# Main neighbour table written in 24-slot pieces in place of eight-slot pieces, in a four-layer GNN and expert kernel

## What is computed

```
x = x + gat2(layernorm(x), src, dst)            # two attention layers over the 100,000 edges, dense by counts
x = x + experts8(layernorm(x))
x = x + layernorm(x) @ W(edge_weight, src, dst) # a 256 x 256 matrix scattered from weights
x = x + experts4(layernorm(x), edge_index)      # gate: 4-head attention over 65,536 other edges
x = x + feature_attention(layernorm(x), src, dst)
x = x + experts6(layernorm(x))
x = x + gat8heads(layernorm(x), src, dst)       # 8-head attention over the 100,000 edges
x = x + experts8b(layernorm(x))
```

## Time and profile before

| | us |
|---|---|
| three timed runs | 5290.30, 5306.82, 5312.11 |
| median | 5306.82 |
| the profiled execution, its own time | 5308.64 |
| span of the profiled execution | 5307.1 |
| mean granted clock of PE in it | 0.876 of full |

### The profile page before, as it was taken

The page is one execution under the profiler, slowest core; times in us unless marked ns, Lnnn a source line. Parts: engine busy times, 40 slices in busy tenths (PEclk is TensorE's granted clock), DMA queues, the critical chain, the costliest instruction groups (busy, mean ns, idle before and its releaser), DMA issues. The chain is left out here.

```text
span 5307.1 us, 71457 instructions
## 1 busy us (share of the span) xinstructions
PE 3317.8 (63%) x17311; PEld 2482.2 (47%) x17312; DVE 3019.0 (57%) x7503; ACT 1600.5 (30%) x2745; POOL 2063.6 (39%) x1895
## 2 busy tenths in 40 slices
PE   0440036499698695277771699868345567777677
PEld 0430036487586584255550244356234445555455
DVE  8886648588588556133335754442444555565563
ACT  0232024376475121133330454322101222222221
POOL 1136300200200252656551200026377877777662
PEclk9999999899898796588885899979677788898899
DMA  0311125443452322211123554422443333333241
GB/s 31 74 19 44 13 82 232 169 153 104 170 159 85 111 67 91 88 27 33 33 38 108 200 170 158 165 91 67 129 91 86 88 86 83 82 84 84 78 76 28
DMA packets 326382, 501.17 MB, mean 94 GB/s; under 512 B 152614, under 2 KB 241005, under 8 KB 324168
## 3 DMA queue, kind: packets, MB, share of 16 engines
q1 hardware_dynamic: 193750, 259.75, 15.6%
q0 software_dynamic: 83888, 189.73, 13.7%
q10 hardware_dynamic: 48578, 49.98, 2.8%
HBM read 367.16 MB, written 137.35 MB: 95 GB/s over the span
## 5 line engine op out<-in xcount | busy, mean ns | idle before, releaser
L2393 POOL DMA_INDIRECT l3a_got<-rows,l3a_idx x832 | 1003.3, 1206 | 356.1 <-issue 257.5
L2469 PE MATMUL ps<-l3a_v,ident 128*128 x2032 | 592.9, 455 | 476.8 <-DVEq L2596 395.3
L2469 PEld LDWEIGHTS ps<-l3a_v,ident 128*128 128x128 f32 x2032 | 452.5, 228 | 614.5 <-issue 522.0
L1659 PE MATMUL ps<-l0a_all_rows,l0a_w 128*128 128x257 f32 x2500 | 559.5, 384 | 38.1 <-DVE l0a_w L1768 37.8
L1659 PEld LDWEIGHTS ps<-l0a_all_rows,l0a_w 128*128 128x128 f32 x2500 | 473.9, 191 | 124.3 <-issue 54.3
L2831 POOL DMA_INDIRECT l1a_got<-rows,l1a_idx x352 | 351.2, 998 | 248.8 <-DVEq L3033 130.0
L2069 PE MATMUL ps<-l2a_table,l2a_count 128*128 128x512 bf16 x1875 | 409.7, 382 | 38.1 <-ACT l2a_count L1994 38.1
L2419 ACT ACT_TABLE_LOAD x90 | 115.5, 1283 | 750.7 <-issue 459.4
L2854 PE MATMUL ps<-xt,l1w_w 128*128 x640 | 225.8, 506 | 169.3 <-ACT l1a_h L2909 74.2
L2069 PEld LDWEIGHTS ps<-l2a_table,l2a_count 128*128 128x128 bf16 x1875 | 183.9, 98 | 264.0 <-issue 46.6
L2590 DVE TENSOR_TENSOR l3a_v<-l3a_got,l3a_p_kept x127 | 291.6, 2296 | 0.0
(11 more groups left out here) (1019 smaller groups left out, 6446.8 us busy)
## 6 DMA issues: line engine op xcount, KB each, us to landing
l0a_held<-counts SPq DMA_DIRECT2D x130, 640.0 KB
counts<-count_held SPq DMA_DIRECT2D x13, 3200.0 KB
l2a_held<-counts SPq DMA_DIRECT2D x65, 640.0 KB
l3a_got<-rows,l3a_idx POOLq DMA_INDIRECT x832
l_y<-l1a_y_sb ACTq DMA_DIRECT2D x20, 640.0 KB
l2a_table<-rows SPq DMA_DIRECT2D x16, 640.0 KB, 5.1
l2a_state<-l1a_fresh ACTq DMA_DIRECT2D x1, 9984.0 KB
l2a_seen<-l2a_state POOLq DMA_DIRECT2D x12, 768.0 KB, 6.0
```

The costliest lines, as they stand in the source:

```text
L1659: ins = pe.matmul(sums_of(n, k, D + 1), w[:, at, k * P:(k + 1) * P], all_rows[:, at, 1:RW], start=(at == 0), stop=(at == HI - 1))
L2393: pool.indirect_dma_start(out=got[:, at:at + RW], out_offset=None, in_=rows[:, :], in_offset=bass.IndirectOffsetOnAxis(ap=idx[:, a, k:k + ...
L2469: ins = pe.matmul(totals, c.ident[:, :], rows_now[:, k, :, :].rearrange("p h d -> p (h d)"), start=(k == 0), stop=(k == ADDED - 1))
```

## The change

`write_table` takes the graph's `fewest` as its piece width. For gate that is 8, as before; for main it is 24. The closing piece has the same width. `whole_row`, the most pieces in a chunk, becomes 64 // 24 = 2 for main. `ell` keeps 24 slots ahead of the 64, in place of 8, and the spare area and the table have room for wider pieces. As 24 is no power of two, `fill` no longer shifts to get the number of pieces: it adds up comparisons (size >= 24, size >= 48), which makes two for main and eight for gate.

```diff
-        self.whole_row = WIDE // SLOTS
+        self.whole_row = WIDE // fewest
...
-        m.ell, m.past = sb("main_ell", [P, NT, SLOTS + WIDE], I32), sb("main_past", [P, NT, WIDE])
+        m.ell, m.past = sb("main_ell", [P, NT, m.fewest + WIDE], I32), sb("main_past", [P, NT, WIDE])
...
         def write_table(eng, s, odd, emptied=None):
+            width = s.fewest
...
                         with eng.Fori(0, n_units) as u:
-                            eng.dma_start(s.table[:, bass.ds(to + u * SLOTS, SLOTS)],
-                                          s.ell[:, bass.ds(t, 1), bass.ds(SLOTS + u * SLOTS, SLOTS)].rearrange("p o s -> p (o s)")).then_inc(s.stored[odd], 16)
+                            eng.dma_start(s.table[:, bass.ds(to + u * width, width)],
+                                          s.ell[:, bass.ds(t, 1), bass.ds(width + u * width, width)].rearrange("p o s -> p (o s)")).then_inc(s.stored[odd], 16)
...
-                    eng.dma_start(s.table[:, bass.ds(to, SLOTS)],
-                                  s.ell[:, bass.ds(t, 1), bass.ds(at, SLOTS)].rearrange("p o s -> p (o s)")).then_inc(s.closed, 16)
+                    eng.dma_start(s.table[:, bass.ds(to, width)],
+                                  s.ell[:, bass.ds(t, 1), bass.ds(at, width)].rearrange("p o s -> p (o s)")).then_inc(s.closed, 16)
...
-                        ch.add(dve.tensor_copy(s.full_i[:, :], last[:, 0, :]))
-                        ch.add(dve.tensor_tensor(s.ends[:, :], last[:, 0, :], left[:, :], ALU.is_equal))
-                        ch.add(dve.tensor_tensor(last[:, 1, :], last[:, 1, :], spare[:, :], ALU.subtract))
+                        ch.add(dve.tensor_tensor(last[:, 1, :], dest[:, :], last[:, 0, :], ALU.add))
+                        ch.add(dve.tensor_scalar(row[:, 0:NT], last[:, 0, :], float(width), None, ALU.is_ge))
                         ch.join()
...
+                        ch.add(dve.scalar_tensor_tensor(last[:, 1, :], last[:, 1, :], -float(width * (c.NT + 1)), s.ends[:, :], ALU.add, ALU.mult))
+                        for u in range(2, s.whole_row + 1):
+                            ch(dve.scalar_tensor_tensor(row[:, 0:NT], last[:, 0, :], float(u * width), row[:, 0:NT], ALU.is_ge, ALU.add))
...
-                        ch.add(dve.tensor_copy(s.ell[:, :, 0:SLOTS], s.ell[:, :, WIDE:SLOTS + WIDE]))
+                        ch.add(dve.tensor_copy(s.ell[:, :, 0:width], s.ell[:, :, WIDE:width + WIDE]))
...
-    columns_of = lambda edges, fewest: edges + (fewest + 2 * SLOTS) * NT + 5 * WIDE
+    columns_of = lambda edges, fewest: edges + 3 * fewest * NT + 5 * WIDE
```

More of the change, by code:

```diff
@@ L134, in __init__ @@
         self.last_entry = entries.shape[0] - 1
-        self.whole_row = WIDE // SLOTS
+        self.whole_row = WIDE // fewest
         self.columns = table.shape[1]
-        self.trash = self.columns - WIDE - 2 * SLOTS * c.NT
+        self.trash = self.columns - WIDE - 2 * fewest * c.NT
         self.chunks = -(-edges // WIDE)
@@ L160, in allot @@
         self.moved = sb("moved", [P, SLOTS, NT])
-        self.full_i, self.last, self.ends = sb("full_i", [1, NT], I32), sb("last", [1, 2, NT]), sb("ends", [1, NT])
+        self.last, self.ends = sb("last", [1, 2, NT]), sb("ends", [1, NT])
         self.last_i = sb("last_i", [1, 2, NT], I32)
@@ L215, in build_graphs @@
         g.raw = part_of(c.xt, NT * P, NT * ENTRY).bitcast(I32).rearrange("p (t e) -> p t e", e=ENTRY)
-        g.ell = part_of(five, 0, NT * (SLOTS + WIDE)).bitcast(I32).rearrange("p (t e) -> p t e", e=SLOTS + WIDE)
-        g.past = part_of(five, NT * (SLOTS + WIDE), NT * WIDE).rearrange("p (t e) -> p t e", e=WIDE)
+        g.ell = part_of(five, 0, NT * (g.fewest + WIDE)).bitcast(I32).rearrange("p (t e) -> p t e", e=g.fewest + WIDE)
+        g.past = part_of(five, NT * (g.fewest + WIDE), NT * WIDE).rearrange("p (t e) -> p t e", e=WIDE)
         sign, bits, bits_i = sb("sign", [P, 8]), sb("bits", [P, 9]), sb("bits_i", [P, 9], I32)
@@ L374, in clear @@
                     ch.add(dve.memset(s.wrote[:, :], 0.0))
-                    ch.add(dve.tensor_scalar(s.spare[:, :], c.iota[0:1, 0:NT], float(SLOTS), float(s.trash), ALU.mult, ALU.add))
+                    ch.add(dve.tensor_scalar(s.spare[:, :], c.iota[0:1, 0:NT], float(s.fewest), float(s.trash), ALU.mult, ALU.add))
                     ch.add(dve.tensor_copy(s.values[:, :, :], c.iota[:, 0:P].unsqueeze(2).broadcast_to([P, P, s.hist])))
@@ L637, in fill @@
                     n = dve.value_load(s.chunk_i[0:1, 0:1], min_val=1, max_val=s.chunks)
-                    ch(dve.memset(s.ell[:, :, WIDE:SLOTS + WIDE], 0))
+                    width = s.fewest
+                    ch(dve.memset(s.ell[:, :, WIDE:width + WIDE], 0))
                     dve.sem_inc(s.emptied, 1)
@@ L646, in fill @@
                         ch.add(dve.tensor_tensor(dest[:, :], scan[:, 0:NT], spare[:, :], ALU.subtract))
-                        ch.add(dve.tensor_tensor(last[:, 1, :], scan[:, 0:NT], left[:, :], ALU.add))
+                        ch.add(dve.tensor_scalar(s.ends[:, :], left[:, :], 1.0, None, ALU.is_ge))
                         ch.join()
-                        ch.add(dve.tensor_copy(s.full_i[:, :], last[:, 0, :]))
-                        ch.add(dve.tensor_tensor(s.ends[:, :], last[:, 0, :], left[:, :], ALU.is_equal))
-                        ch.add(dve.tensor_tensor(last[:, 1, :], last[:, 1, :], spare[:, :], ALU.subtract))
+                        ch.add(dve.tensor_tensor(last[:, 1, :], dest[:, :], last[:, 0, :], ALU.add))
+                        ch.add(dve.tensor_scalar(row[:, 0:NT], last[:, 0, :], float(width), None, ALU.is_ge))
                         ch.join()
-                        ch.add(dve.tensor_scalar(s.full_i[:, :], s.full_i[:, :], SLOTS.bit_length() - 1, None, ALU.logical_shift_right))
-                        ch.add(dve.scalar_tensor_tensor(last[:, 1, :], last[:, 1, :], -float(SLOTS * (c.NT + 1)), s.ends[:, :], ALU.add, ALU.mult))
+                        ch.add(dve.scalar_tensor_tensor(last[:, 1, :], last[:, 1, :], -float(width * (c.NT + 1)), s.ends[:, :], ALU.add, ALU.mult))
+                        for u in range(2, s.whole_row + 1):
+                            ch(dve.scalar_tensor_tensor(row[:, 0:NT], last[:, 0, :], float(u * width), row[:, 0:NT], ALU.is_ge, ALU.add))
                         ch.join()
-                        ch.add(dve.tensor_copy(row[:, 0:NT], s.full_i[:, :]))
                         ch.add(dve.tensor_tensor(last[:, 1, :], last[:, 1, :], spare[:, :], ALU.add))
+                        ch.add(dve.tensor_scalar(s.has[:, :], row[:, 0:NT], 1.0, None, ALU.is_ge))
                         ch.join()
-                        ch.add(dve.tensor_scalar(s.has[:, :], row[:, 0:NT], 1.0, None, ALU.is_ge))
                         ch.add(dve.tensor_scalar(row[:, 0:NT], row[:, 0:NT], 1.0, None, ALU.max))
-                        ch.add(dve.tensor_scalar(last[:, 1, :], last[:, 1, :], float(SLOTS * c.NT), None, ALU.add))
+                        ch.add(dve.tensor_scalar(last[:, 1, :], last[:, 1, :], float(width * c.NT), None, ALU.add))
                         ch.join()
```

6 lines of the change are left out of this document (3 added, 3 removed).

## The result

| | before | after |
|---|---|---|
| median of 6 runs each on one chip, us | 5305.8 | 5268.2 |
| ratio, 95% interval | | 0.9937 [0.9919, 0.9954] |
| span of the profiled execution, us | 5307.1 | 5267.7 |

The changed kernel takes 5268.2 us where 5272 was forecast: 33 us less than before by the ratio (24 to 43 by its interval).

A forecast was written before the change was run, and what follows sets the result against it. The prediction took SP's queue, by its issuing of small DMAs, to set the stage's end. Its terms, -34.6 us of issue and +0.4 of DVE, gave 5306.8 - 34.2 = 5272.6, stated as 5272, range 5252 to 5294.

The forecast's parts named there:

- Step 1: Main's pieces on SP's queue: 49 become 14, so 35 fewer at the quiet 1.00 us each, -35.0 us.
- Step 2: SP's main pieces and closings: beside POOL's indirect DMAs the queue works at rate 0.40, giving -34.6 us.
- low bound of 0.30: SP's main pieces: rate if tile heads fare worse beside POOL's DMAs; gain 28, or 26 with longer overlap at gate.
- Step 3: SP's gate pieces meet the same 30 us of POOL's DMAs, so the shift stays -34.6; ACT's queue costs 0.
- Step 4: Closings, waits and empty blocks: counts unchanged, the 2.9 us wait for main's closings stays; 0.
- Step 5: Main's pieces grow from 128 x 32 to 128 x 96 bytes; taken as 0 us.
- Rival A: Each removed piece on SP's queue is worth its average 1.99 us: gain 70 us, time 5237; chance 0.05.
- Step 6: DVE's `fill(m)` handles 24 slots in place of 8: +0.4 us; `fill(g)`'s added comparisons stay covered by a wait, 0.
- Step 7: SP stays last by far, its stage ending about 688.5 us; first instruction of `count` at 687 to 692.
- B: Gathers of places overlap SP's gate pieces fully, main's heads run at 0.25; gain 20 to 25, time 5284; chance 0.08.
- C: PE's clock behind the stage: less idle brings more 1.2 GHz time; within noise, chance 0.10, or slower (5333), 0.04.
- sign of being wrong: The stage ends less than 26 us earlier, or it does end that much earlier and the total does not follow.

The follow-up runs named there:

- pieces8: Changed kernel with main pieces of 8 slots again (49 on SP, 43 on ACT), closings and layout as changed; ratio 1.0014 to the kernel before.
- the repeats: Kernel before and changed kernel, each unchanged, profiled once more on one chip; stage ends at 719.2 and 694.4 us, no timed ratio.
- the two measurements: The changed kernel timed against the kernel before, then word for word again on another chip; ratios 0.9937 and 0.9948.
- no_place: Changed kernel without POOL's 25 gathers of places, DVE copying c.node into c.place instead; ratio 0.9912 to the kernel before.
- double_place: Changed kernel with POOL's 25 gathers of places issued twice, writing the same values; ratio 0.9995 to the kernel before.
- the swapped kernel: Changed kernel with ACT writing gate's even tiles and SP the odd ones, run twice; ratios 0.9925 and 0.9927 to the kernel before.
- ranks_first: Changed kernel with ACT's DMA of gate's ranks ahead of ACT's pieces of main, not behind its closings; ratio 0.9952 to the kernel before.

## Why the prediction was right, and where its steps were off

**Step 1, the pieces.** Right: 14 and 12 pieces, and a stage that follows their number (723.0, 700.6, 692.1). The prices were right to 0.1 us at gate wherever POOL is silent: 35.22 us for 17 gate pieces in two runs, and 26.6 for 13 closings in all eleven with SP's full share.

**Step 2, the rate of 0.40.** Right in its result, wrong in its parts. The last main piece was predicted at 547.5 and came at 556.9, outside the 545 to 556 that I named. The last closing was predicted at 588.0 (in place of 622.6, both starts) and came at 589.9; its row ends at 560.07 + 30.21 = 590.3. Three things lie behind the 9.4 us. SP's first piece came 16.3 us after its release at 485.7, in place of 9.0 (485.4 to 494.4) before, which is some 7. The prediction took 505:521 as quiet, but in the trace before, POOL's fetches for gate begin at 516.6, and POOL is busy 5.10 us of that window:

```profile
505.00:521.00 16.00, 0.60 (x2) 0.17 (x2) 7.90 (x48) 0.00 (x0) 5.10 (x4) 1.00 0.19 15
```

With the true edges and the rate worked out anew, the same steps give 549 to 551 in place of 547.5. And beside those fetches the work that was left moved more slowly than 0.40 allows. The closings gave most of it back: they began later, in less loud time, and took 29.9 us to the start of the last, where the steps had 37.4. My 0.40 was a mean over pieces and heads; the low bound of 0.30 "if tile heads fare worse" was nearer for main, where the 55.3 us hold 32.3 of quiet work beside 34.5 us of fetches (a loss of 0.67 for each us, a rate of 0.33). That tile heads are the reason is not shown.

**Step 3, the same loud time at gate.** This is the term that was mis-sized. L285 came at 576.8 us (577 predicted), the place gathers at 594.7 (596), gate's first piece at 602.6 (597, where the prediction's own shift of 34.6 gives 601.3), ACT's end at 655.6 (658). The prediction let the gate stretch keep "the same 30 loud us". Its own numbers say otherwise: before, SP's gate work began at 628.0, 5 us into the gathers; 34.6 us earlier it would begin ahead of them and meet all 33 us. In the runs the gathers overlap gate's pieces for 25.6 us after the change and for 20.2 before it, and each such us costs 0.77 to 0.8 us. The pieces took 54.8 us in place of 51.4. Along SP's queue the shift is 32.6 us at the last main closing, 33.3 at gate's first piece and 29.9 from gate's last piece to the end. That is the gap of 4.3 us to the predicted 34.2: 1.6 by the last closing, 0.7 given back in between, 3.4 at gate.

**Step 4, waits.** Half right. The wait stayed, but grew from 2.9 to 6.5 us: SP's last closing now ends 13.5 us after the ranks DMA is issued, where it was 19.1, and in both kernels the wait ends some 3 us after the ranks have landed. What lay between the last closing and gate's first piece was nevertheless 12.3 us in place of 13.0, so it cost nothing in the sum.

**Step 5, bytes.** Right: no run shows a cost, and pieces of three times the bytes kept the quiet issue length (a median of 348 ns in both kernels). Rival A, 70 us by the average price, is out. The Trainium skill, "DMA: Bandwidth & Descriptors", section "Anatomy of one DMA — SWDGE (gpsimd) path", gives a fixed cost of about 2.0 us for a DMA that GpSimd issues; charged to SP's queue it would have made the same 70 us. The gain of about 30 us for 35 pieces, and the 1.00 us between two pieces of a tile, show that it is not charged there.

**Step 6, DVE.** The mechanism was as told, the size too small. DVE's copy of the closing slots took 0.47 us in place of 0.25, and the first half of main was ready at 485.6 against 485.3 (485.6 to 486.8 in the three executions after, 483.9 and 485.3 in the two before). The cover of `fill(g)` stood: 13.0 us of waiting left.

```profile
467.50 0.47 DVE L674 COPY graphs_main_ell<-graphs_main_ell 128x600 int32<-128x600 int32 x1
```
```profile
533.43 0.79 DVE L680 COPY graphs_five<-xt 128x832 int32<-128x832 int32 x1 [13.01 <-DMA xt<-entries_gate,graphs_gate_at_i]
```

But pieces8, which has this part, 1.25 us of added comparisons and no fewer pieces, ended the stage 3 us later than the kernel before and was 0.14% slower. I counted DVE's own time and not what a later start may do beside POOL's DMAs: in the ten executions in which the main data was ready after 485 us, the first piece came 9 to 18.5 us behind it, in the other four after 3.5 to 8. Why, is not shown.

**Step 7, the next late one.** Right: SP stays last. The first instruction of `count` came at 693.5, just outside the predicted 687 to 692.

**The rivals.** B (loud stretches take more, 20 to 25 us) was closer to the truth in its mechanism than its chance of 0.08 says: the gain of the stage, 27.5 us over the repeats, lies between it and the forecast. C did not come: the clock's fall is as deep and as late behind the start of PE's work as before. The forecast of the total, 34.2 us, lies within the 24 to 43 and the 19 to 37 of the two measurements. That it met the first one's 33 so closely is in part luck: the stage, which is all that the forecast was built from, gave 27.5, not far above the 26 that the prediction named as its sign of being wrong, and the pair of repeats alone (24.8) lies below it.

## What to carry to other kernels

Here a queue that issues many small DMAs from a register loop was priced by its instructions, not by its bytes: 1.0 us for a further piece, and 2.6 for a tile with its two register loads and one piece, of 8 slots or of 24. Fewer and wider pieces give back just that, as long as the queue is the last to arrive. Before moving such a queue, lay POOL's indirect DMAs over its timeline: a us of them cost SP's queue 0.77 to 0.91 us beside the gathers of places and 0.67 beside gate's fetches, so they belong where the queue waits anyway. And an average price (1.99 us here) mixes quiet time, loud time and tile heads, and overpriced this change twofold.

## What was not expected of the hardware

**Queues slow down beside POOL's indirect DMAs, register instructions too, and at times nearly stop.** The rows of line L244 on SP's queue of the changed kernel, in 485:503 (25 DMAs of POOL in 466:500) and then for ten gate tiles in 632:660, with no POOL DMA:

```profile
L244 SPq TENSOR_LOAD <-graphs_main_trips_i x1: 1335/1335/1335, 485.9 to 485.9; - x1
L244 SPq FUSED_REGOPS  x1: 702/702/702, 488.0 to 488.0; - x1
L244 SPq SEQ_ASSERT  x1: 700/700/700, 490.1 to 490.1; - x1
```
```profile
L244 SPq TENSOR_LOAD <-graphs_gate_trips_i x10: 270/275/277, 632.2 to 655.4; - x10
L244 SPq FUSED_REGOPS  x10: 158/161/164, 632.5 to 655.7; - x10
L244 SPq SEQ_ASSERT  x10: 18/18/18, 632.8 to 656.0; - x10
```

An assertion on a register, which moves no data, takes 700 ns in place of 18, and the next instruction starts 1.4 to 2.1 us after the one before. What the two share is not shown; no run here tests it. Nor is the loss one number. Main's 13 closings in the changed kernel took 3.6 us over their quiet 26.6 beside seven indirect DMAs (564.1 to 573.3), at most 0.4 for each us. On ACT's queue, the 14 gate pieces took 48.5 us beside 33.5 us of place gathers and 30.0 with none (no_place), or 0.55 for each us. The Trainium skill, "DMA: Bandwidth & Descriptors", section "SWDGE vs HWDGE vs iDMA", calls DMAs issued from SP or ACT immune to the interference between DVE and GpSimd's descriptors. The runs here don't contradict that narrow sentence, but whoever reads it as "GpSimd's DMAs cannot slow SP's" is wrong by 0.87 us for each us in double_place.

**One kernel, two starts.** The thirteen register instructions ahead of SP's first issue took 3.4 us in one execution of the swapped kernel and 16.3 in another, both beside POOL's writes of gate records. In the quick one SP went on to seven main pieces while those writes ran until 506.5:

```profile
486.82 23.55 SPq L247 DMA_DIRECT2D table_main<-graphs_main_ell  x7
```

Their quiet price is 5 x 2.58 + 1.00 + 0.35 = 14.3 us, so each us beside the writes cost about 0.5. It goes with when SP is released (483.4 and 486.6 us); what decides it stays open.

**Four-byte writes delay their neighbours.** The 3200 words of ranks land 17.7 us after their issue (19.1 before), and the closings that fly beside them are waited for 5.2 us (no_place) and 6.5 (after) in place of 0.8 (ranks_first).
